# Soft mixture of experts, combine stage: who adds the negative maxima to the logits of steps 24 to 63

## The reference, cut to what matters

```python
logits = (jnp.einsum('tzd,ed->tze', x, phi_w) + phi_b).reshape(t, z, n, p)
D = jax.nn.softmax(logits, axis=3)
C = jax.nn.softmax(logits, axis=2)
X_tilde = jnp.einsum('tznp,tzd->npd', D, x)
...
Y = jnp.einsum('tznp,npH->tzH', C, Y_tilde)
```

## Time and profile before

| what | value |
|---|---|
| median of 3 runs | 791.04 us (785.99 to 792.75) |
| the profiled execution's own time | 791.13 us |
| its span | 789.4 us |
| busy share of the span: PE, DVE, ACT, POOL | 83%, 60%, 46%, 43% |
| mean granted clock of PE | 0.903 |
| steps 0 to 39 of the combine loop | 674.75 to 756.50 us |

### The profile page before, as it was taken

One profiled execution on the slowest core, in us unless ns is written; L12 is line 12 of the kernel. 1 busy time (PEld: TensorE's weight loads), 2 busy tenths in 40 slices (PEclk: granted clock), 3 DMA queues, 4 the chain that ended last, 5 costly groups with the idle time before them and its releaser, 6 DMA issues. The chain is left out here.

```text
span 789.4 us, 17996 instructions
## 1 busy us (share of the span) xinstructions
PE 656.1 (83%) x7326; PEld 373.9 (47%) x7326; DVE 475.5 (60%) x1242; ACT 359.4 (46%) x633; POOL 340.2 (43%) x368
## 2 busy tenths in 40 slices
PE   3598989999869999798828860799989879999995
PEld 1314545555427988677724430333333344444442
DVE  6556757785263334261375869699999861424455
ACT  3604646666657335242337431655445454334410
POOL 3004646666520000000015351299989927856531
PEclk9956979999788999898778995799999989999999
DMA  4523240000036400000019000000000000000000
GB/s 87 95 68 47 56 61 10 4 4 4 2 138 199 99 12 4 3 2 4 5 35 360 14 1 0 0 0 1 1 0 0 1 1 1 0 1 13 1 13 27
DMA packets 18389, 27.17 MB, mean 34 GB/s; under 512 B 3699, under 2 KB 16948, under 8 KB 17284
## 3 DMA queue, kind: packets, MB, share of 16 engines
q1 hardware_dynamic: 17390, 25.82, 13.0%
q10 hardware_dynamic: 918, 0.21, 0.2%
HBM read 18.11 MB, written 1.05 MB: 24 GB/s over the span
## 5 line engine op out<-in xcount | busy, mean ns | idle before, releaser
L491 ACT ACTIVATE at_exp<-at_psum 128x512 f32<-128x512 f32 x136 | 78.2, 606 | 62.3 <-PE at_psum L608 59.8
L1592 POOL TENSOR_TENSOR all_phi_b<-all_phi_b,mo_work 128x512 f32<-128x512 f32 x56 | 71.0, 1268 | 44.5 <-ACT mo_work L1798 40.1
L838 POOL TENSOR_TENSOR all_x<-all_x,ff_x_blocks 128x512 f32<-128x512 f32 x3 | 3.9, 1286 | 170.4 <-ACT ff_x_blocks L1029 170.4
L1613 PE MATMUL all_psum<-all_phi,mo_xt 128*128 128x512 f32 x128 | 66.1, 643 | 7.3 <-ACT mo_work L1780 5.6
L306 POOL TENSOR_SCALAR_AFFINE_SELECT at_exp<-at_exp 128x512 f32<-128x512 f32 x68 | 43.1, 634 | 63.9 <-ACT at_exp L491 63.9
L1562 POOL TENSOR_TENSOR mo_work<-mo_work,mo_max 128x1024 f32<-128x1024 f32 x32 | 61.4, 1920 | 21.3 <-DVE mo_max L1854 21.3
L363 DVE TENSOR_REDUCE at_neg_max<-at_psum 128x2 f32<-128x512 f32 x68 | 47.0, 691 | 33.6 <-PE at_psum L595 33.5
L1646 PE MATMUL all_psum<-mo_xt,all_phi_centred 128*128 128x512 f32 x128 | 66.2, 598 | 0.0
L1798 ACT ACTIVATE mo_work<-all_psum 128x512 f32<-128x512 f32 x64 | 37.7, 601 | 61.8 <-PE all_psum L1646 61.8
L595 PE MATMUL at_psum<-at_k_stack,at_q_stack 49*128 49x256 bf16 x272 | 59.1, 306 | 6.2 <-DMA at_k_stack<-at_part_l 3.2
L1699 PE MATMUL all_psum<-mo_work,mo_y_slots 128*128 128x512 f32 x128 | 62.5, 595 | 1.8 <-DVE mo_work L1902 1.8
(11 more groups left out here) (346 smaller groups left out, 1329.6 us busy)
## 6 DMA issues: line engine op xcount, KB each, us to landing
all_expert_w<-in_expert_w SPq DMA_DIRECT2D x1, 4096.0 KB, 18.1
ff_b_up<-in_b_up SPq DMA_DIRECT2D x1, 2048.0 KB, 9.7
ff_a_up<-in_a_up SPq DMA_DIRECT2D x1, 2048.0 KB, 14.1
ff_w_down<-in_w_down SPq DMA_DIRECT2D x2, 1024.0 KB, 18.7
at_q_stack<-at_part_h SPq DMA_DIRECT2D x24, 64.0 KB
at_k_stack<-at_part_h SPq DMA_DIRECT2D x24, 64.0 KB
at_q_stack<-at_part_m SPq DMA_DIRECT2D x16, 64.0 KB
at_k_stack<-at_part_m SPq DMA_DIRECT2D x16, 64.0 KB
```

The costliest lines, as they stand in the source:

```text
L491: nc.scalar.activation(e[:, m // 2, 2 * (m % 2):2 * (m % 2) + 2, :, :].rearrange("p h j q -> p (h j q)"), psum[:, ST + n % 3, :], ACT.Exp, ...
L1592: nc.gpsimd.tensor_tensor(tot[:, ch % 2, :], first, ec[:, ch % 2, j, :], ALU.add).then_inc(added, 1)
L1613: last = nc.tensor.matmul(psum[:, 2 * hf + k, :], xt[:, P * z:P * z + P], phi_d[:, HALF * hf + W * k:HALF * hf + W * k + W], start=True, s ...
```

## The change

From step 24 on the bf16 matmul (L1645) is left out of `combine_logits`. In its place the negative maxima of chunks 1, 2 and 3 are spread once each by one matmul (`spread_max`) into bank 3 of PSUM and copied by ACT to `max_spread` in SBUF (`take_spread`), between steps 11 and 16. DVE has a new function `lower(n)`: it adds `max_spread` to the logits in PSUM and writes the sum to `ec`; ACT then takes the exponential in place in SBUF. PE's wait for a free bank becomes a wait for `lower`. `lower(m + 24)` stands in DVE's list ahead of `scale` of step m, and `invert_total(ch + 1)` moves to between j = 12 and j = 13 of the chunk before.

```diff
--- before.py
+++ after.py
@@ -1492,8 +1492,12 @@
     NJ, NCH = SL // P, T // W
     NC = NJ * NCH
     LEAD = 24
+    by_dve = [n for n in range(NC) if n >= LEAD]
+    before = lambda n: sum(k < n for k in by_dve)
     with ExitStack() as ctx:
         a = Alloc(nc, ctx, "mo")
+        max_spread = a.sb("max_spread", [P, 3, W])
+        spread_done, spread_ready, lowered = (a.sem(k) for k in ("neg_max_spread", "neg_max_ready", "lowered"))
         psum = s["psum"]
         phi, phi_d, ew, eb, selp, blk = (s[k] for k in ("phi_centred", "phi", "expert_w", "expert_b", "sel_slot", "same_slot"))
         xs_t, spare = phi_d, s["phi_b"]
@@ -1635,15 +1639,25 @@
 
                 def combine_logits(n):
                     ch, j = n // NJ, n % NJ
-                    if n >= 3:
+                    if n >= 3 and n - 3 in by_dve:
+                        pe.wait_ge(lowered, before(n - 3) + 1)
+                    elif n >= 3:
                         pe.wait_ge(ec_ready, n - 2)
                     else:
                         pe.wait_ge(lc_ready, U)
                     if j == 0 and ch % 2 == 0:
                         pe.wait_ge(mp_ready, ch // 2 + 1)
                     cols = slice(W * ch, W * ch + W)
-                    nc.tensor.matmul(psum[:, n % 3, :], selp[:, :], mp_t[:, cols], start=True, stop=False)
-                    nc.tensor.matmul(psum[:, n % 3, :], phi[:, P * j:P * j + P], xt[:, cols], start=False, stop=True).then_inc(cl_done, 1)
+                    if n not in by_dve:
+                        nc.tensor.matmul(psum[:, n % 3, :], selp[:, :], mp_t[:, cols], start=True, stop=False)
+                    nc.tensor.matmul(psum[:, n % 3, :], phi[:, P * j:P * j + P], xt[:, cols], start=n in by_dve, stop=True).then_inc(cl_done, 1)
+
+                def spread_max(k):
+                    if k == 0:
+                        pe.wait_ge(mp_ready, 2)
+                    else:
+                        pe.wait_ge(spread_ready, k)
+                    nc.tensor.matmul(psum[:, 3, :], selp[:, :], mp_t[:, W * k + W:W * k + 2 * W], start=True, stop=True).then_inc(spread_done, 1)
 
                 def natural(q):
                     pe.wait_ge(xs_ready, q + 1)
@@ -1670,7 +1684,7 @@
 
                 def total(ch):
                     if ch == 0:
-                        pe.wait_ge(mp_ready, 2)
+                        pe.wait_ge(spread_ready, 3)
                     else:
                         pe.wait_ge(rc_ready, ch)
                     pe.wait_ge(added, (NJ - 1) * (ch + 1))
@@ -1730,6 +1744,8 @@
                     for _ in range(k):
                         combine_logits(n)
                         n += 1
+                        if n in (12, 14, 16):
+                            spread_max(n // 2 - 6)
                         if n % NJ == 5 and n > NJ:
                             total(n // NJ - 1)
                         if n % NJ == 7 and n > NJ:
@@ -1789,13 +1805,22 @@
 
                 def combine_exps(n):
                     ch, j = n // NJ, n % NJ
+                    part = ec[:, ch % 2, j, :]
+                    if n in by_dve:
+                        act.wait_ge(lowered, before(n) + 1)
+                        nc.scalar.activation(part, part, ACT.Exp).then_inc(ec_ready, 1)
+                        return
                     act.wait_ge(cl_done, n + 1)
                     if n == NJ:
                         act.wait_ge(d_ready, U)
                         act.wait_ge(slot_maxed, U)
                     if ch >= 2:
                         act.wait_ge(y_done, n - 2 * NJ + 1)
-                    nc.scalar.activation(ec[:, ch % 2, j, :], psum[:, n % 3, :], ACT.Exp).then_inc(ec_ready, 1)
+                    nc.scalar.activation(part, psum[:, n % 3, :], ACT.Exp).then_inc(ec_ready, 1)
+
+                def take_spread(k):
+                    act.wait_ge(spread_done, k + 1)
+                    nc.scalar.copy(max_spread[:, k, :], psum[:, 3, :]).then_inc(spread_ready, 1)
 
                 def take_y(ch):
                     act.wait_ge(y_done, NJ * ch + NJ)
@@ -1831,6 +1856,8 @@
                     combine_exps(n)
                     if n == 7:
                         take_maxima(1)
+                    if n in (11, 13, 15):
+                        take_spread((n - 11) // 2)
                     if n % NJ == LEAD % NJ - 1 and n > LEAD:
                         take_y((n - LEAD) // NJ)
                     if n % NJ == LEAD % NJ + 2 and n > LEAD + NJ:
@@ -1894,6 +1921,15 @@
                     if ch >= 1:
                         dve.wait_ge(rt_done, ch)
                     v.reciprocal(rc[:, :], psum[:, 3, 0:P]).then_inc(rc_ready, 1)
+
+                def lower(n):
+                    ch, j = n // NJ, n % NJ
+                    dve.wait_ge(cl_done, n + 1)
+                    if n == by_dve[0]:
+                        dve.wait_ge(spread_ready, 3)
+                    if ch >= 2:
+                        dve.wait_ge(y_done, n - 2 * NJ + 1)
+                    v.tensor_tensor(ec[:, ch % 2, j, :], psum[:, n % 3, :], max_spread[:, ch - 1, :], ALU.add).then_inc(lowered, 1)
 
                 def scale(ch, j):
                     if j == 0:
@@ -1946,9 +1982,13 @@
                 take_back(3)
                 slot_values(2)
                 slot_values(3)
+                invert_total(0)
                 for ch in range(NCH):
-                    invert_total(ch)
                     for j in range(NJ):
+                        if NJ * ch + j + LEAD in by_dve:
+                            lower(NJ * ch + j + LEAD)
+                        if j == 13 and ch + 1 < NCH:
+                            invert_total(ch + 1)
                         scale(ch, j)
                         if j == 5 and ch >= 1:
                             finish(ch - 1)
```

## The result

The changed kernel takes 860.3 us (median of 4 runs, 849.75 to 861.37) against 791.89 us before (4 runs): a ratio of 1.0947, 95% interval 1.0875 to 1.102. It is slower by about 68 us; 853 was predicted, with a range of 840 to 886. The ratios in this document compare the fast runs of a kernel with the fast runs of the kernel before that were taken beside them, so they are not always the quotient of the two medians.

The account below looks back on a forecast made before the run. PE's work was taken to bound the kernel before; afterwards PE and DVE alternate. Loop +59.5 us, end +0.3 and low clock +2 gave +61.8 on 791.13, so 853 us, range 840 to 886.

Parts of the forecast that it names:

- What bounds the kernel before: Combine loop, steps 0 to 39: PE busy 80.32 of 81.75 us, never waiting because DVE is ahead; 1.94 us a step.
- The order decides: Combine loop: scaling of step m waits behind the addition for step m + 24, so PE and DVE alternate each step.
- the signs that the prediction named: Combine loop: DVE releases each combine, PE idles 1.3 to 1.5 us, pace 3.3 to 3.4 us, POOL idle about half.
- The size of a round: Combine loop: 1.98 + 0.04 + 0.60 + 0.74 us make 3.36 us a step in place of 1.94.
- Combine 0 to combine 39: Combine loop: 39 rounds take 131.0 us, and once-per-chunk work adds 5.7 us.
- Once-per-chunk work: Combine loop: total and spread hidden; transposes 0.88, reciprocals 1.92, two normalisations 2.9 us; together 5.7 us.
- The clock: PE in the loop: full clock mostly holds, one low spell +2 us; rival of falling clock 883 or 915 us, 16%.
- by the page the time would be 883 us or more: Combine loop: the skill page's repeated clock loss would make each of 40 rounds a short group; rival's chance 16%.
- Combine 0 came 1.1 us sooner: Loop start: the first combine matmul moves from 674.75 to 676.73 us, +1.98.
- the stretch behind the last total: Kernel's end: nothing changes behind POOL's last addition; the tail of 32.9 us has no additions.

Follow-up runs that it names:

- two places of lead: Changed kernel with DVE's scaling of step m behind the addition of step m + 22 instead of m + 24: 786.51 us, ratio 1.0012 to before.
- The doubled addition: Changed kernel with a second, same-size addition into a scratch tile before each of DVE's 40: 916.34 us, ratio 1.1716 to before.
- the kernel one place ahead: Changed kernel with DVE's scaling of step m behind the addition of step m + 23 instead of m + 24: 792.92 us, ratio 1.0151 to before.
- half an addition more: Changed kernel with a second, half-width addition (256 of 512 columns) before each of DVE's 40: 865.63 us, ratio 1.1019 to before.

## Why the prediction was right

**What bounds the kernel before: right.** PE had no gap and DVE was far ahead.

**The order decides: right, and shown from both sides.** The cause is that the scaling stands behind an addition that waits for logits just issued. Taking that order away by one place brought 60 of the 62 us back; bringing it into the kernel before, without additions, cost 51. The work of the 40 additions by itself costs little: with two places of lead the loop has them all and runs at PE's pace, but for 1.04 us at each of two normalisations. Of the signs that the prediction named one was off: POOL was idle two thirds of the loop (48.70 of 137.55 us busy), not half.

**The size of a round: right.** 3.36 us reckoned from four rows, 3.36 measured; PE's pause 1.38 us in both. The reason is that both hand-overs had already occurred in the trace of before, though rarely. Combine 0 to combine 39: 136.7 us reckoned, 137.55 measured. The difference is one stretch at the low clock: from 782.82 us one round took 4.29 us.

**Once-per-chunk work: right.** PE's stop at each normalisation is 2.83 us in the changed kernel, 1.38 + 1.46 = 2.84 reckoned. Total and spread are hidden in PE's pause.

```profile
758.47 1.12 PE L1713 MATMUL all_psum<-mo_work,mo_y_slots 128*128 128x512 f32 x2 [2.83 <-DVE mo_work L1938]
...
815.96 1.13 PE L1713 MATMUL all_psum<-mo_work,mo_y_slots 128*128 128x512 f32 x2 [2.83 <-DVE mo_work L1938]
```

**The clock: right for this kernel, too mild as a judgement.** It held in the plain rounds and fell after a reciprocal and at the end:

```profile
782.82 1.12 PE L1713 MATMUL all_psum<-mo_work,mo_y_slots 128*128 128x512 f32 x2 [2.19 <-DVE mo_work L1938]
783.79 1.82 PE L1653 MATMUL all_psum<-mo_xt,all_phi_centred 128*128 128x512 f32 x2
785.40 1.91 PE L1702 MATMUL all_psum<-mo_rtotal,all_from_group 128*128 128x128 f32 x8
```

In the loop that cost under 1 us, 4.29 - 3.36. Behind the last total PE works without a wait at a clock of 0.50, up to 828.20 us (the row of 824.00 above), and the stretch to the end is 2.9 us longer than before. Together that is some 3.7 us against the 2 that I had set. I had placed the risk at the normalisations; the fall came after the stop at the second reciprocal (2.19 us) and after the stop at the last total (1.67 us). That the clock holds at a pause of 1.38 us a round was right, with little room: at 1.71 us it still held, at 1.98 us the loop's mean was 0.69.

The Trainium skill ("TensorE: Matmul & The Clock Gate", HAM oscillation) describes groups of matmuls of about 2 us between waits of 3 to 5 us, each of which starts at the low clock again. The prediction left the length of these waits out when it said that by the page the time would be 883 us or more: a pause of 1.38 us is far shorter, and the changed kernel kept its clock (0.99). The doubled addition shows the same kind of loss (0.69), and already at a pause of 1.98 us.

**The miss of 7 us** between 853 and 860 is not in the loop: 6.1 us of it lie ahead of this layer, in code that is the same, at a mark that moves by 12 us from profile to profile. One of the four runs of the changed kernel took 849.75 us. In the layer itself +62.4 us were measured against +61.8 reckoned, and that this is so close is partly luck. Combine 0 came 1.1 us sooner after the mark than reckoned (+0.9 for +2.0), for a reason that I have not found, and the stretch behind the last total was 2.9 us longer where nothing was reckoned but the 2 us of clock.

## What to carry to other kernels

Before an instruction is put into an engine's list, ask what it waits for and what stands behind it. If what stands behind it is needed by the other engine before that engine can produce the next thing waited for, the two engines take turns, whatever room their busy shares show. A lead of one place in the list took 60 of 62 us of this away here, and a second place 5 us more. Where PE already pauses in each round, more work on the other engine can cost more than its length, because the clock may fall as well: here 24 us of additions cost 63 us, while 13 us of them cost 13.

## What the runs showed of the hardware that I had not expected

In these loops the clock's fall was not in proportion to the pause. With the same matmuls in each round, pauses of 1.38 and 1.71 us left the loop's granted clock at 0.99, and 1.98 us brought it to 0.69 and the loop 40 us more. Three bf16 matmuls in the pause, whose results nobody read, gave the 40 us back. The length of a single stop did not decide by itself. After 2.83 us the changed kernel's matmuls came at full clock both times (1.12 and 1.13 us for a pair); after 2.76 us those of the kernel one place ahead, whose PE had worked almost without a gap until then, came at the low one both times (2.08 and 2.07 us). The changed kernel stopped 2.19 us at each of its two reciprocals: behind the first, at 726.26 us, the logits took 1.02 us, behind the second, at 782.82, 1.82. With half an addition more even 3.16 us left the full clock (a pair of 1.12 us), and in the changed kernel the 1.67 us at the last total were followed by the low one. What decides between them is open.
